# Layer 0 of the next group moved beside the MLP of this one, between the pieces of its second product

## The chip, the cores and the metric

The kernel runs on one core of a Trainium2 chip. The metric is the device time of one execution in microseconds. The runs of the kernel before took 2260.58 to 2263.42 us, with a median of 2262.15.

## The reference

Four layers follow one another on x (64 batches of 64 rows and 256 columns), with a context of the same shape:

```python
def layer0(x_c, x_s):            # channels are the 64 rows, times the 256 columns
    Mn = Wn @ inorm(x_c) + bn;  Mm = Wm @ inorm(x_s) + bm
    A = softmax(Mn.T @ Mm)       # 256 x 256 for each batch
    return Wo @ ((Wl @ x_s + bl) @ A.T) + bo + x_c
def layer1(x, c):                # 32 query heads over 8 key heads of width 8
    return layernorm(softmax(q(x) k(c).T / sqrt(8) + mask) v(c) @ Wo + bo + x) * gamma + beta
def layer2(c, latents):          # 16 heads of width 16, 128 keys: context and latents
    h = attention(latents, concat(c, latents), mask) @ out_w + out_b + latents
    return gelu(rmsnorm(h) @ mlp_w1 + b1) @ mlp_w2 + b2 + latents
def layer3(x, state):            # a recurrence over the 64 rows, 32 heads of 8 x 8
    mixes -> w, k, v, r, g;  s = k v + w s;  out = r (u k v + s_before)
    x1 = x + groupnorm(out) * g @ Wo.T
    return x1 + sigmoid(xr @ Wfr.T) * (relu(xk @ Wfk.T) ** 2 @ Wfv.T)
```

## The kernel before

All is computed in f32. The 64 batches are cut into 8 groups of 8 (512 rows, four tiles of 128 rows). A group passes through layers 0, 1, 2 and the MLP in one block, and through layer 3 in the block after it: group_block(now, before, after) works on layers 0 to 2 of group `now`, on layer 3 of group `before`, and loads the input of group `after`. The blocks are (0, none, 1), then a hardware loop over groups 1 to 6, then (7, 6, none), and (none, 7, none), which holds layer 3 alone. At the end of each block all engines meet, and POOL clears the semaphores.

In a block every engine has its instructions in program order, and the order is written out by hand. A counter of steps runs from 0. Layer 3 is cut into stages (moments, normalize, turn, shift, maa, five mixes with the products between them, 16 scans, center, variance, gate, project and the feed forward stages), and the dictionary `due` gives each a step: the first at 0, the scans at 27 to 42, center at 46, variance at 48, gate at 50, project at 52, the last at 64. The function step() issues the stages due at the present step. Around it, the four steps at the start hold layer 0's first products (mm, mn, ml and the transposes of the context, cT). The loop `for i in range(END)` follows. layer0(i) has eight units of softmax at i = 0 to 7 and their transposes and values up to i = 14. Layer 1's 16 units begin at i = A1 = 14, layer 2's 16 units at A2 = 35, and END is 61. Then come the MLP, eight pieces of the first product (line 579, Gelu at line 936), and the second product as two tiles of four rows of pieces (line 906), with a step after each.

A unit of layer 1 or 2 is a score product (line 714), masked (DVE, 1337), largest (DVE, 1343), subtract (POOL, 1502), exp (ACT, 1049), transposes (855) and a drain (1055, 1057). Four units make a pair (lines 869 and 874), whose totals are inverted by ACT (1067, 1069), divided (DVE, 1358), projected (579) and added (DVE, 1367). A unit of layer 0 is nmax (DVE, 1300), two exponents with sums (ACT, 1039), rden (DVE, 1304), scaling of one half on POOL (1510) and one on ACT (1111), transposes (729), a copy (1310), value (738) and the output product with Wo. Layer 3's scan n is a product on POOL (1464), a column copy (1466), the scan (DVE, 1179), a read-out (DVE, 1191) and a product with `pick` (656).

PSUM has eight banks in three rings: "score" (2 banks: scores of all layers), "turn" (4 banks: all else of layers 0 to 2 and the MLP) and "late" (2 banks: layer 3). fill() waits until the bank's last content was drained, in program order. The input of the next group is loaded by ACT's queue (load_ahead) at the end of layer 2, and its statistics and normalization (normalize_ahead, on DVE, with deviations_ahead on ACT) follow behind the Gelus. The ACT function tables are switched by tables(), line 921, among logarithm and exponent, tanh and exponent, and Gelu.

Of the kernel before, what the change touches and what calls it, by code (L numbers as in the profile page):

```python
# [25 lines left out]
NB = 8  # L26
# [27 lines left out]
def build(nc, a, out):  # L54

    with ExitStack() as ctx:
# [115 lines left out]
        edge = sb("edge", [128, 2, KT, NB])  # L172
        stats3 = sb("stats3", [128, NP, 6])
# [28 lines left out]
        mn = cut(early, 1024, NP, E)  # L202
        mm0 = cut(early, 4096, NP, E)
        mlT = cut(early, 2048, NP, 2, 128)
        mo = cut(early, 3072, NP, E)
# [71 lines left out]
        def normalize_ahead(dve, link):  # L277
# [10 lines left out]
            dve.sem_inc(sig("stats0_ready"), 1)  # L288
            dve.wait_ge(sig("rstd0_ready"), 1)
# [6 lines left out]
        with nc.Block() as block:  # L296
# [137 lines left out]
            def _(dve):  # L434
# [10 lines left out]
                normalize_ahead(dve, link)  # L445
# [70 lines left out]
        A1 = U0 + 6  # L516
        A2 = A1 + UNITS + 5
        END = A2 + UNITS + 10

# [10 lines left out]
        def group_block(now, before, after):  # L530
# [18 lines left out]
            with nc.Block() as block:  # L549
# [22 lines left out]
                def _(pe):  # L572
# [110 lines left out]
                    if now is None:  # L683
                        rest()
                        return


                    step()
                    for q in range(2):
                        product(("mm", q), 512, [(conv["Wm"][:, :], ch[:, 2 * q:2 * q + 2, :])])  # L690
                    for q in range(2):
                        product(("mn", q), 512, [(conv["Wn"][:, :], xh0[:, 2 * q:2 * q + 2, :])])
                    step()
                    for q in range(2):
                        t, full = fill(pe, "turn", ("ml", q))
                        for p in range(2):
                            for s in range(2):
                                ins = mm(t[:, 256 * p + 128 * s:256 * p + 128 * s + 128], c0[:, 2 * q + p, 128 * s:128 * s + 128],
                                         conv["Wl"][:, :], start=True, stop=True)
                        ins.then_inc(full, 1)  # L700
                    step()
                    flip("cT", c0)
                    step()
# [38 lines left out]
                    def layer0(i):  # L742
                        if i < U0 and i % 2 == 0:
                            scores0(i // 2)
# [18 lines left out]
                    def keys1():  # L763
                        pe.wait_ge(sig("cT_ready"), KT)
# [47 lines left out]
                    def between(i):  # L812
                        if i == U0 + 2:
                            keys1()
                        if i == U0 + 6:
                            values1()
                        for h in range(2):
                            if i == 4 * h + 11:
                                pe.wait_ge(sig("x1_ready"), 2 * h + 2)
                                turn_half("x1T", x0, h)  # L820
                            if i == 4 * h + 12:
# [61 lines left out]
                    for i in range(END):  # L883
                        step()
                        layer0(i)
# [10 lines left out]
                    pe.wait_ge(sig("xnT_ready"), 2 * KT)  # L896
                    for n in range(HID // 128):
                        product(("u", n), 512, [(w1[:, k, 128 * n:128 * n + 128], xnT[:, :, k, :]) for k in range(KT)])
                        step()
                    for q in range(2):  # L900
                        t, full = fill(pe, "turn", ("y2", q))
                        for p in (2 * q, 2 * q + 1):
                            for k in range(HID // 128):
                                if p == 0:
                                    pe.wait_ge(sig("gT_ready"), k + 1)
                                ins = mm(t[:, E * (p % 2):E * (p % 2) + E], gT[:, k, 128 * p:128 * p + 128], w2[:, k, :],  # L906
                                         start=k == 0, stop=k == HID // 128 - 1)
                        ins.then_inc(full, 1)
                        step()
# [3 lines left out]
                def _(act):  # L913
# [101 lines left out]
                    if now is None:  # L1015
# [3 lines left out]

                    for q in range(2):  # L1020
                        t, free = take(act, ("mm", q))
                        link(af(mm0[:, 2 * q:2 * q + 2, :].rearrange("p n t -> p (n t)"), t[:, :], ACT.Identity, bias=v("bm")))
                        act.sem_inc(free, 1)
                        act.sem_inc(sig("mm_ready"), 1)
                    step()
                    step()
                    step()
                    for k in range(KT):
                        drain(("cT", k), hT[:, k, :, 0, :], lambda t: batches(t[:, :]), ACT.Identity, "cT_ready")
                    step()  # L1030
# [40 lines left out]
                    def between(i):  # L1071
                        for h in range(2):
                            r = slice(2 * h, 2 * h + 2)
                            if i == 4 * h + 11:
# [27 lines left out]
                    for i in range(END):  # L1102
# [3 lines left out]
                        if i < U0:  # L1106
                            exps0(i)
                        if 1 <= i < U0 + 1:
                            act.wait_ge(sig("rden0_ready"), i)
                            s = soft[:, (i - 1) % SOFT, 256:512]  # L1110
                            af(s, s, ACT.Identity, scale=rden0[:, i - 1, 1:2]).then_inc(sig("p0b_ready"), 1)
# [5 lines left out]
                    if after is not None:  # L1117
                        load_ahead(act, after, lambda: act.wait_ge(sig("xnT_ready"), 2 * KT), lambda: act.wait_ge(sig("xr3_ready"), NP))
                    tables(GELU)
                    for n in range(HID // 128):  # L1120
                        drain(("u", n), gT[:, n, :], lambda t: t[:, :], ACT.Gelu_apprx_tanh, "gT_ready", bias=v("b1", n))
                        step()
                    if after is not None:
                        tables(LOG_EXP)
                        deviations_ahead(act, link)
                    for q in range(2):
                        step()
                    rest()
                    if after is not None:
# [3 lines left out]
                def _(dve):  # L1133
# [143 lines left out]
                    if now is None:  # L1277
# [3 lines left out]

                    step()
                    for q in range(2):
                        t, free = take(dve, ("mn", q))
                        link(ts(flat(mn[:, 2 * q:2 * q + 2, :]), t[:, :], v("bn"), None, ALU.add))
                        dve.sem_inc(free, 1)
                        dve.sem_inc(sig("mn_ready"), 1)
                    step()
                    for q in range(2):
                        t, free = take(dve, ("ml", q))  # L1290
                        link(nc.vector.tensor_copy(mlT[:, 2 * q:2 * q + 2, :, :].rearrange("p n s o -> p (n s o)"), t[:, :]))
                        dve.sem_inc(free, 1)
                        dve.sem_inc(sig("ml_ready"), 1)
                    step()
                    step()

# [272 lines left out]
```

## Time and profile before

| | |
|---|---|
| median of the runs | 2262.15 us |
| profiled execution | 2263.65 us |
| its span | 2261.9 us |
| mean granted clock of TensorE | 0.931 |
| TensorE matmul busy | 1812.2 us (80%) |
| VectorE busy | 1396.9 us (62%) |
| ScalarE busy | 874.9 us (39%) |
| GpSimd busy | 851.3 us (38%) |
| table loads on ScalarE | 55, of 1283 ns each |

An engine is busy while it computes; waits and DMA issues are not counted. The span runs from the first to the last instruction. The granted clock is the share of full speed at which TensorE was run.

### The profile page before, as it was taken

Reading aid. Unit: us, or ns where it says so; the run is one execution under the profiler, and the core shown is the slowest. Engines: PE = TensorE matmul, PEld = TensorE weight load, DVE = VectorE, ACT = ScalarE, POOL = GpSimd, SP = SyncE. Lnnn points to the kernel's source line nnn. Section 1 sums busy time; section 2 is a strip of 40 time slices with the busy share of each in tenths; the row PEclk is TensorE's granted clock in tenths of the full one; section 3 lists DMA queues with packets and bytes.
Section 4 is the critical chain, followed back from the end, with each engine's and each line's share of the span. In section 5 each row is a group of like instructions: output and inputs, shape, how many; then the busy total and the mean of one; then the engine's idle time right before and its main releaser. Section 6 shows DMA issues by size and latency. Waiting matters only on the chain. (4 is left out here: it accounts for less than half of the span.)

```text
span 2261.9 us, 31481 instructions
## 1 busy us (share of the span) xinstructions
PE 1812.2 (80%) x10801; PEld 1095.3 (48%) x10801; DVE 1396.9 (62%) x2337; ACT 874.9 (39%) x1680; POOL 851.3 (38%) x896
## 2 busy tenths in 40 slices
PE   3888877988778787887878878788877888788765
PEld 2465434654356443564445634465434654356413
DVE  3663578635876368754687446873578645875273
ACT  1444442533425334353333533254432543426202
POOL 3531256303752037411374114730266203742060
PEclk9999998999989899998998989999999999989967
DMA  5000011010210102010020101201011010200030
GB/s 155 1 1 24 7 39 39 1 40 1 53 24 2 39 1 63 14 34 8 15 62 1 34 7 26 51 1 40 1 42 35 1 39 1 62 15 10 2 76 9
DMA packets 73515, 60.84 MB, mean 27 GB/s; under 512 B 38888, under 2 KB 56440, under 8 KB 73336
## 3 DMA queue, kind: packets, MB, share of 16 engines
q1 hardware_dynamic: 49592, 41.70, 8.5%
q10 hardware_dynamic: 23200, 16.85, 2.5%
q8 instruction: 98, 1.61, 0.3%
q14 instruction: 81, 0.66, 0.1%
q0 software_dynamic: 544, 0.03, 0.0%
HBM read 20.28 MB, written 4.19 MB: 11 GB/s over the span
## 5 line engine op out<-in xcount | busy, mean ns | idle before, releaser
L1502 POOL TENSOR_TENSOR soft_ring<-soft_ring,seg_max 128x512 f32<-128x512 f32 x256 | 326.7, 1284 | 495.9 <-DVE seg_max L1343 495.8
L1049 ACT ACTIVATE soft_ring<-soft_ring 128x512 f32<-128x512 f32 x256 | 160.9, 628 | 413.3 <-POOL soft_ring L1502 406.8
L656 PE MATMUL bank<-late,pick 128*128 128x512 f32 x256 | 160.8, 715 | 99.9 <-DVE late L1191 99.7
L1337 DVE SCALAR_TENSOR_TENSOR soft_ring<-bank,mask 128x512 f32<-128x512 f32 x256 | 164.6, 684 | 105.0 <-PE bank L714 94.4
L1464 POOL TENSOR_TENSOR late<-late 128x520 f32<-128x520 f32 x128 | 197.4, 1542 | 71.2 <-DMA late<-late 49.9
L1179 DVE TENSOR_TENSOR_SCAN late<-late 128x520 f32<-128x520 f32 x128 | 188.0, 1468 | 9.3 <-DVE xr L1367 2.2
L1343 DVE TENSOR_REDUCE seg_max<-soft_ring 128x8 f32<-128x512 f32 (+1 forms) x256 | 169.4, 677 | 8.9 <-DVE early L1400 1.9
L1510 POOL TENSOR_SCALAR soft_ring<-soft_ring,rden 128x256 f32<-128x256 f32 x64 | 59.1, 924 | 305.3 <-DVE rden L1304 305.3
L855 PEld LDWEIGHTS bank<-ident,soft_ring 128*128 128x128 f32 x1024 | 121.5, 147 | 108.2 <-issue 86.8
L714 PE MATMUL bank<-early 64*128 64x512 f32 (+1 forms) x512 | 123.3, 583 | 58.6 <-ACTq L1042 55.2
L855 PE MATMUL bank<-ident,soft_ring 128*128 128x128 f32 x1024 | 164.4, 290 | 5.8 <-ACT soft_ring L1049 5.5
L579 PE MATMUL bank<-late,maa 128*128 128x512 f32 (+1 forms) x224 | 126.1, 680 | 23.4 <-DVEq L1171 19.3
L579 PE MATMUL bank<-wo,early 128*128 128x256 f32 x512 | 130.2, 399 | 11.0 <-DVEq L1361 10.9
L1191 DVE TENSOR_TENSOR late<-late 128x512 f32<-128x512 f32 x128 | 135.8, 1061 | 0.3 <-PE bank L656 0.3
L921 ACT ACT_TABLE_LOAD x55 | 70.6, 1283 | 163.4 <-issue 102.9
L579 PE MATMUL bank<-early,w 128*128 128x512 f32 x256 | 113.6, 602 | 7.4 <-ACT early L1098 7.4
L656 PEld LDWEIGHTS bank<-late,pick 128*128 128x128 f32 x256 | 46.5, 216 | 150.2 <-DVE late L1191 108.6
L579 PEld LDWEIGHTS bank<-wo,early 128*128 128x128 f32 x512 | 97.9, 199 | 32.5 <-DVEq L1361 14.3
L906 PE MATMUL bank<-w,early 128*128 128x256 f32 x512 | 111.8, 379 | 0.0
L936 ACT ACTIVATE early<-bank,vec 128x512 f32<-128x512 f32 x96 | 66.0, 687 | 107.1 <-PE bank L579 104.3
L906 PEld LDWEIGHTS bank<-w,early 128*128 128x128 f32 x512 | 97.3, 190 | 16.6 <-issue 3.8
L714 PEld LDWEIGHTS bank<-early 64*128 64x128 f32 x512 | 48.9, 211 | 113.6 <-issue 111.9
(242 smaller groups left out, 3390.1 us busy)
## 6 DMA issues: line engine op xcount, KB each, us to landing
late<-late SPq DMA_DIRECT2D x128, 260.0 KB, 3.0
c<-in_ctx ACTq DMA_DIRECT2D x8, 512.0 KB, 3.8
x<-in_x ACTq DMA_DIRECT2D x8, 512.0 KB, 6.0
out_x<-late SPq DMA_DIRECT2D x8, 512.0 KB, 4.9
mask<-in_mask_Bx1xSxS_ff ACTq DMA_DIRECT2D x16, 128.0 KB, 4.8
w<-in_L_xattn_mlp_w ACTq DMA_DIRECT2D x2, 1024.0 KB
mask<-in_mask_BxS_ik SPq DMA_DIRECT2D x8, 256.0 KB, 3.5
wkv<-in_L_xattn_kv_w ACTq DMA_DIRECT2D x1, 512.0 KB
```

Of the source, the lines that this page charges most:

```text
L579: ins = mm(t[0:lhsT_cols(lhsT), 0:cols], lhsT, rhs, start=n == 0, stop=n == len(terms) - 1)
L656: mm(t[:, :], pick[:, j, :], rs[:, j % 2, :], start=j == 0, stop=j == HS - 1).then_inc(full if j == HS - 1 else sig("rs_used"), 1)
L714: ins = mm(t[:, width * n:width * n + width], lhsT, rhs, start=True, stop=True)
L855: ins = tr(t[:, 128 * n:128 * n + 128], soft[:, u % SOFT, 128 * n:128 * n + 128], ident[:, :])
L906: ins = mm(t[:, E * (p % 2):E * (p % 2) + E], gT[:, k, 128 * p:128 * p + 128], w2[:, k, :], start=k == 0, stop=k == HID // 128 - 1)
L1049: af(soft[:, u % SOFT, :], soft[:, u % SOFT, :], ACT.Exp).then_inc(sig("exp"), 1)
L1179: nc.vector.tensor_tensor_scan(sj[:, n % 2, :], wP[:, k, :, :].rearrange("p b t -> p (b t)"), aj[:, n % 2, :], 0.0, ALU.mult, ALU.add).the ...
L1191: tt(batches(rs[:, n % 2, :]), batches(rT[:, k, :]), sj[:, n % 2, :].rearrange("p (b t) -> p b t", t=LP)[:, :, 0:L], ALU.mult).then_inc(si ...
L1337: stt(out=cuts(u, soft[:, u % SOFT, :]), in0=cuts(u, t[:, :]), scalar=HD1 ** -0.5 if u < UNITS else 1.0 / HD2, in1=mask.unsqueeze(1).broad ...
L1343: nc.vector.tensor_reduce(seg_max[:, u % SOFT, 0:KVH if u < UNITS else 4], cuts(u, soft[:, u % SOFT, :]), X, ALU.max).then_inc(sig("max"), 1)
L1464: tt(aj[:, n % 2, :], kP[:, k, :, :].rearrange("p b t -> p (b t)"), vj[:, n % 3, :], ALU.mult).then_inc(sig("kv_done"), 1)
L1502: tt(s, s, seg_max[:, u % SOFT, 0:segs].unsqueeze(2).broadcast_to([128, segs, 512 // segs]), ALU.subtract).then_inc(sig("sub"), 1)
```

## The change

The block no longer starts with layer 0. A block works on layers 1 and 2 and the MLP of `now`, on layer 3 of `before` and on layer 0 of `after`. Layer 1's units begin at i = A1 = 3 and A2 is 24, END 50; the keys, values and queries of layer 1 stand at i = 0 to 2. After that come 25 slots, each with one step(): slots 0 to 7 hold a piece of the first MLP product, slots 8 to 15 half of a row tile of the second (four of eight terms each, one bank for each row tile in place of one for two), and layer 0 of the next group has its first products at slots 7 to 9 and its units from slot 10 on. The stages of layer 3 keep their steps, so gate (step 50) now falls into slot 0. The statistics of the next input are taken at slot 4 and its normalization at slot 6. Tiles mn, mlT and mo have other places so that they don't share memory with gT. POOL copies two columns of the context's transpose to `edge_now` at the start of a block, since layer 0 now overwrites them in it, and ACT waits for that. A block (none, none, 0) with layer 0 alone of group 0 comes first. The waits on x1_ready and cT_ready are gone, since the border of the block lies between.

```diff
-        A1 = U0 + 6
+        A1 = 3
         A2 = A1 + UNITS + 5
         END = A2 + UNITS + 10
+        HIDDEN = HID // 128
+        AHEAD = 10
+        SLOTS = AHEAD + U0 + 7
+        def slots(now, after):
+            if after is None:
+                return range(2 * HIDDEN + 1)
+            return range(AHEAD - 3 if now is None else 0, SLOTS)
...
# TensorE
+                        if i == -3:
+                            if now is not None:
+                                pe.wait_ge(sig("ahead_ready"), 2 * NP)
+                            (products mm and mn)
+                        if i == -2: (products ml)
+                        if i == -1:
+                            flip("cT", c0)
...
-                        if i == U0 + 2:
+                        if i == 0:
                             keys1()
-                        if i == U0 + 6:
+                        if i == 2:
                             values1()
...
+                    def hidden_out(p, late_half):
+                        if not late_half:
+                            fill(pe, "turn", ("y2", p))
+                        b, _ = place["y2", p]
+                        for k in range(4 * late_half, 4 * late_half + 4):
+                            if p == 0:
+                                pe.wait_ge(sig("gT_ready"), k + 1)
+                            ins = mm(banks[b][:, 0:E], gT[:, k, 128 * p:128 * p + 128], w2[:, k, :], start=k == 0, stop=k == HIDDEN - 1)
+                        if late_half:
+                            ins.then_inc(sig(f"bank{b}_full"), 1)
+                    for s in slots(now, after):
                         step()
+                        if now is not None and s < HIDDEN:
+                            hidden(s)
+                        if now is not None and HIDDEN <= s < 2 * HIDDEN:
+                            hidden_out((s - HIDDEN) // 2, s % 2)
+                        if after is not None:
+                            layer0(s - AHEAD)
...
# ScalarE
+                    for s in slots(now, after):
                         step()
+                        if now is not None and s < HIDDEN:
+                            tables(GELU)
+                            drain(("u", s), gT[:, s, :], lambda t: t[:, :], ACT.Gelu_apprx_tanh, "gT_ready", bias=v("b1", s))
+                        if now is not None and after is not None and s == 6:
+                            tables(LOG_EXP)
+                            deviations_ahead(act, link)
+                        if after is not None:
+                            layer0(s - AHEAD)
...
# VectorE
+                    for s in slots(now, after):
                         step()
+                        if now is not None and after is not None:
+                            if s == 4:
+                                statistics_ahead(dve, link)
+                            if s == 6:
+                                normalize_ahead(dve)
+                        if now is not None and s % 2 == 0 and HIDDEN + 2 <= s <= 2 * HIDDEN:
+                            hidden_added((s - HIDDEN) // 2 - 1)
+                        if after is not None:
+                            layer0(s - AHEAD)
...
+        group_block(None, None, 0)
         group_block(0, None, 1)
```

## Rows read from the trace of the kernel before

**Rows 1.** Timeline of TensorE, first product of four blocks: start us, us, engine, line, [idle before].
```profile
44.84 2.19 PE L579 MATMUL bank<-early,conv_Wm 128*128 128x512 f32 x3 [2.28 <-PEq L483]
...
227.27 1.95 PE L579 MATMUL bank<-early,conv_Wm 128*128 128x512 f32 x4 [1.98 <-PEq L483]
...
495.85 2.07 PE L579 MATMUL bank<-early,conv_Wm 128*128 128x512 f32 x2 [6.11 <-issue]
...
767.22 1.22 PE L579 MATMUL bank<-early,conv_Wm 128*128 128x512 f32 x1 [6.03 <-issue]
```

**Rows 2.** Windows of one turn of the loop; columns in the first line.
```profile
core 0: us, PE busy (x) PEld busy (x) DVE busy (x) ACT busy (x) POOL busy (x), PEclk, DMA share, GB/s
495.90:595.50 99.60, 82.63 (x421) 41.53 (x422) 59.47 (x107) 41.29 (x89) 32.57 (x32) 0.93 0.07 14
595.50:671.00 75.50, 56.02 (x303) 34.03 (x302) 65.39 (x84) 21.30 (x40) 55.32 (x48) 0.91 0.18 41
...
676.70:733.40 56.70, 49.67 (x498) 38.37 (x496) 33.72 (x61) 35.30 (x67) 12.80 (x16) 1.00 0.01 1
733.40:761.20 27.80, 27.79 (x96) 18.13 (x96) 8.27 (x28) 8.57 (x12) 0.36 (x2) 1.00 0.23 67
```

**Rows 3.** Line 1179 (the scans) in two windows: duration ns min/median/max, first and last start.
```profile
L1179 DVE TENSOR_TENSOR_SCAN late<-late x12: 1230/1407/1760, 593.1 to 636.3; 128x520 f32<-128x520 f32 x12
...
L1179 DVE TENSOR_TENSOR_SCAN late<-late x4: 1225/1230/1231, 645.9 to 660.9; 128x520 f32<-128x520 f32 x4
```

**Rows 4.** Windows of the first block, up to layer 1's scores and from there on.
```profile
44.80:84.50 39.70, 29.19 (x179) 19.05 (x179) 17.98 (x36) 16.44 (x46) 10.85 (x12) 0.83 0.03 8
84.50:195.90 111.40, 92.51 (x888) 64.27 (x887) 67.51 (x119) 56.16 (x109) 47.40 (x52) 0.98 0.00 1
```

**Rows 5.** Groups by line and form, one turn: busy us, mean ns | idle before.
```profile
L1337 DVE SCALAR_TENSOR_TENSOR soft_ring<-bank,mask 128x512 f32<-128x512 f32 x32 | 20.6, 685 | 14.4 <-PE bank L714 13.1 <-DVE early L1358 0.9 <-DVE xr L1367 0.3
L855 PE MATMUL bank<-ident,soft_ring 128*128 128x128 f32 x128 | 20.4, 289 | 0.6 <-ACT soft_ring L1049 0.6
...
L579 PE MATMUL bank<-wo,early 128*128 128x256 f32 x64 | 16.3, 400 | 1.4 <-DVEq L1361 1.4
...
L1343 DVE TENSOR_REDUCE seg_max<-soft_ring 128x4 f32<-128x512 f32 x16 | 10.5, 677 | 0.6 <-DVE late L1197 0.2 <-DVE early L1358 0.2
L714 PE MATMUL bank<-early 64*128 64x512 f32 x32 | 9.4, 662 | 0.4 <-DVE soft_ring L1337 0.4
...
L809 PE MATMUL bank<-wkv,hT 128*128 128x256 f32 x32 | 7.6, 388 | 0.0
...
L579 PE MATMUL bank<-hT,wkv 128*128 128x512 f32 x16 | 7.2, 593 | 0.0
L1350 DVE TENSOR_TENSOR qring<-early,hmask 128x512 f32<-128x512 f32 x8 | 6.8, 857 | 1.1 <-DVE early L1415 0.5 <-DVE early L1358 0.2 <-DVE xr L1367 0.2
...
L869 PE MATMUL bank<-early,ones 128*32 128x256 f32 x64 | 4.3, 385 | 0.0
...
L1264 DVE SCALAR_TENSOR_TENSOR late<-late,vec 128x512 f32<-128x512 f32 x4 | 2.8, 748 | 0.1
```

**Rows 6.** Timeline of TensorE at the end of layer 2 in the first block.
```profile
186.24 1.12 PE L874 MATMUL bank<-early,ones 128*32 128x128 f32 x32
187.14 1.13 PE L874 MATMUL bank<-early 128*32 128x128 f32 x32
...
194.26 0.66 PE L760 MATMUL bank<-ident,c 128*128 128x128 f32 x4 [2.50 <-DVE c L1380]
195.85 1.22 PE L579 MATMUL bank<-early,w 128*128 128x512 f32 x1 [0.93 <-ACT early L1098]
```

**Rows 7.** Timeline of ScalarE behind the last Gelu, and of VectorE for the next input.
```profile
748.29 1.28 ACT L921 ACT_TABLE_LOAD   x1 [0.19 <-ACT early L936]
...
480.02 1.38 DVE L292 TENSOR_SCALAR early<-x,mv,rstd 128x256 f32<-128x256 f32 x4
```

**Rows 8.** Line 1502 (subtract): first block, and layer 2 units beside scans.
```profile
L1502 POOL TENSOR_TENSOR soft_ring<-soft_ring,seg_max x32: 1038/1042/1417, 88.6 to 177.9; 128x512 f32<-128x512 f32 x32
...
L1502 POOL TENSOR_TENSOR soft_ring<-soft_ring,seg_max x7: 1040/1899/1902, 646.0 to 674.8; 128x512 f32<-128x512 f32 x7
```

More of the change, by code:

```diff
@@ L682, in _ @@
                     step, rest = beside(layer3)
-                    if now is None:
+                    if now is None and after is None:
                         rest()
                         return
[L688 to L703, printed above, removed]
                     HALVES = (slice(0, 64), slice(64, 128))
@@ L881, in project @@
                         product(("out", c), E, [(attended[:, c % 2, n, :], wo1[:, n, :] if c < NP else wo2[:, n // 2, n % 2, :]) for n in range(4)])
-                    for i in range(END):
+                    for i in range(END) if now is not None else ():
                         step()
-                        layer0(i)
                         if unit(i) >= 0 and unit(i) % 2 == 0:
@@ L1100, in between @@
                                 act.sem_inc(free, 1)
-                    for i in range(END):
+                    for i in range(END) if now is not None else ():
                         step()
@@ L1105, in _ @@
                             turned(unit(i - 3))
[L1106 to L1111, printed above, removed]
                         between(i)
@@ L1420, in between @@
                                 one_query(b)
-                    for i in range(END):
-                        layer0(i)
+                    for i in range(END) if now is not None else ():
                         if unit(i) >= 0 and unit(i) % 2 == 0:
@@ L1489, in _ @@
                     step, rest = beside(layer3)
-                    if now is None:
+                    if now is None and after is None:
                         rest()
                         return
-                    for _ in range(4):
-                        step()
+                    if now is not None:
+                        for s in range(2):
+                            ins = nc.gpsimd.tensor_copy(edge_now[:, s, :, :], hT[:, :, :, 0, s])
+                        link(ins)
+                        pool.sem_inc(sig("edge_saved"), 1)
                     def subtract(u):
@@ L1503, in subtract @@
                            ALU.subtract).then_inc(sig("sub"), 1)
-                    for i in range(END):
+                    for i in range(END) if now is not None else ():
                         step()
-                        if i < U0:
-                            pool.wait_ge(sig("rden0_ready"), i + 1)
-                            s = soft[:, i % SOFT, 0:256]
-                            ts(s, s, rden0[:, i, 0:1], None, ALU.mult).then_inc(sig("p0_ready"), 1)
                         if unit(i) >= 0:
```

164 lines of the change are left out of this document (82 added, 82 removed).

## The prediction

> **What bounds the kernel now.** I read the windows of one turn of the loop first, then the timeline of TensorE at the block borders, then durations by line. One turn lasts 767.22 - 495.85 = 271.4 us [rows 1]. In the windows [rows 2] TensorE is busy 82.6 of the first 99.6 us (83%), 56.0 of the 75.5 us from 595.5 to 671 (74%), 49.7 of the 56.7 us up to the MLP (88%), and all of the 27.8 us of the MLP; then 6.03 us of nothing stand ahead of the next turn [rows 1]. VectorE has 65.4 of 75.5 us in the window of the scans and about 60% in the windows on both sides of it. So there are three kinds of stretch: TensorE alone (the MLP), VectorE (the scans), and stretches in which in-order queues wait for each other with TensorE at 83 to 88%. About 50 us of a turn find TensorE idle; no work leaves the kernel, so the change can only gain from these 50 us.
>
> **What moves.** Layer 3 keeps its due steps (0 to 64, the scans at 27 to 45), but a turn now counts: steps 0 to 49 are layers 1 and 2, steps 50 to 74 the MLP slots, with layer 0 of the next group from slot 7. Before, steps 0 to 17 held layer 0, layer 1's units ran at steps 18 to 33 and layer 2's at 39 to 54. Now they run at 3 to 18 and 24 to 39. I price five stretches of a turn, each from one event to the next. Before they were 97.2 (start to the first scan, 593.1), 67.8 (first to last scan start, 660.9 [rows 3]), 72.5 (to the MLP, 733.4), 27.8 and 6.0.
>
> **Stretch 1, start to the first scan.** Layer 0 leaves. Alone in the first block it and some 3.7 us of keys and queries keep TensorE busy 29.2 us at a granted clock of 0.83 [rows 4], so I take 24 us for it. In come, up to step 26, seven more units' scores (9.4 x 7/16 = 4.1), ten more turned units (20.4/32 = 0.64 each, 6.4), three more pairs (two products of 1.07 each, 6.4), four output projections (16.3/8 each, 8.1), half of layer 2's keys and values (3.6 + 3.8), its queries at half the keys' work (1.8), a pair of transposes (0.7) and two pairs of layer 2 scores (at layer 1's 9.4/8 each, 2.3) [rows 5]: 37.1 us. Groups that follow each other overlap in the rows (one starts at 186.24 and takes 1.12, the next starts at 187.14 [rows 6]); some 25 groups by 0.1 to 0.2 us, and I take 35 net. TensorE then has 82.6 - 24 + 35 = 94 us of work here. Its share is between what this stretch has now, 83%, and the 88% of the window before the MLP [rows 2], where units, pairs and layer 3 products also share the steps. I take 88%, the nearer in mix of work, since the ping-pong of layer 0 over two score banks has left: 94/0.88 = 107, less the 2.4 us by which the first scan starts before 595.5: 104.5, and 105 with a start in which keys, transposes and queries wait for one another. Bounds: 96.5 (a share of 95%, well above any mixed window) and 111 (83%). So +8.
>
> **Stretch 2, the scans.** VectorE sets it: 67.8 us here. Of its other work between scan 0 and scan 15 there were ten units, now 13: +3 x (0.685 + 0.677) = +4.1; two more spread queries (0.857 each) +1.7; a divide, an add and some normalizing less, about -3.0 (lighter instructions than a unit each) [rows 5]. Net +2.8, and with the 8% that the stretch lasts beyond its own list, 71. Bounds: 68 and 75.
>
> **Stretch 3, last scan to the MLP.** Before, the end of layer 3 (center to the last product) filled the waits of layer 2's end. Now layer 2 ends at step 49 with only center and variance beside it. In the first block, where nothing else runs, the last pair product starts at 186.24 and the MLP at 195.85: 9.6 us of chain (totals, divide, project, add, square, table load, root, scale, transpose, drain) [rows 6]. Ahead of it stand two bare scan steps (4 us); inside it 3.9 us of center and variance on TensorE and ScalarE, in order ahead of the projection and of the last drain. Sum 17.5; bounds 13.6 and 20. So -55.
>
> **Stretch 4, the slots.** TensorE's work is the MLP, 27.8 [rows 2], layer 3's Wo, Wfk, Wfr and Wfv (each twice one MLP piece of 27.8/16 = 1.74, 14 in all, and 1.2 for transposes) and layer 0's 24, for a sum of 67. Two stalls come in. First, slot 7: layer 0's first products wait for the normalized inputs, whose deviation sits in ScalarE's queue behind the Gelu of piece 6. Table load 1.28 and two short activations 0.5, then eight normalizations 2.8 [rows 7], against 2.8 us of TensorE work in between (a transpose stage and piece 7): after the semaphores some 2 to 3.5 us. Second, slots 8 to 10: the context's second transpose needs a bank that holds the first MLP output, and VectorE drains it only behind a shift stage (six instructions of about 0.75, 4.4 [rows 5]) and two copies (1.4): some 2 us. Against that, slots 16 to 24 hold the tail of layer 0: exponent, scaling, transpose, copy, value, output, of which TensorE fills the most; some 2.5 us are bare. 67 + 3 + 2 + 1 = 73 to VectorE's last add; bounds 67 and 80. The extra table loads (Gelu, logarithm, Gelu, logarithm, tanh in the slots, and totals between tanh stages) are about six of 1.28; ScalarE, near 40% busy, hides them except in slot 7. Before, layer 0 was not here, so +45. The copies of the edge (POOL, 0.8) lie beside waits and cost nothing; if not, 0.8.
>
> **Stretch 5, the border.** Barrier and clear stay: 5.5 from VectorE's last instruction.
>
> **Sum.** 105 + 71 + 17.5 + 73 + 5.5 = 272, against 271.4: the idle time changes place rather than size. +0.6 for each of seven groups (six turns and the last full block): +4.2.
>
> **The ends.** A block with layer 0 of group 0 alone is new. The first block before lasted 227.27 - 44.84 = 182.4 us [rows 1], of which 39.7 up to layer 1's scores and 111.4 from there to the MLP [rows 4]. After: layer 0 alone 37.2 + a border of 2.3; then a start of 10.5, again 111.4, slots without layer 3 60, border 2: 223.4, or +41. The block of the last group has no layer 0 beside its MLP: 24 us of work, both stalls and a bit of tail, -30.3. Ends together +10.7.
>
> The profiled execution took 2263.65 (span 2261.9 and 1.75 around it), the runs' median is 2262.15. I add to the median: 2262.15 + 10.7 + 4.2 = 2277. Break-even is a turn shorter by 10.7/7 = 1.5 us. Forecast: slower by 0.7%.
>
> **Rivals.**
> (a) Faster. Layer 0 fits into the slots without either stall (-5.5) and center and variance hide in layer 2's closing chain (-3.9): a turn of 262.6, -8.8 x 7 + 10.7, so 2211. For it: the closing chain leaves TensorE gaps of 2.50 and 0.93 us in the first block [rows 6] into which 3.9 us nearly fit. Against it: layer 3's pieces stand in the queue at fixed places. It decides from a turn below 269.9.
> (b) Two engines over one path. Layer 2's subtract on POOL takes 1.042 us when no scan runs and 1.899 us (median) beside scans [rows 8]; scans beside layer 2 units start (660.9 - 645.9)/3 = 5.0 us apart, the first twelve, mostly beside layer 1 units or none, 3.93 apart [rows 3]. With all 13 units beside scans now layer 2's: 13 x 5.0 + 2 x 2.8 + 4.3 of other work = 75 in place of 71, a turn of 276, and 2262.15 + 10.7 + 32 = 2305. Against it: the five-microsecond steps also carry layer 2 preparations already counted.
> The Trainium skill (SBUF — State Buffer, section "SBUF: two separate sides") says that VectorE with two SBUF inputs and GpSimd lock a shared port pair for a whole instruction and the loser blocks. The stretched subtract agrees with it.
> (c) Crowding. Mixes, layer 1 units and pairs in the same steps keep TensorE at 83% as over all of the present stretch: 111, a turn of 278, and 2319. For it: a masked score ahead of a mix in VectorE's queue delays both bank rings. Against it: layer 0's ping-pong has left, and most of today's gap in this stretch lies before its layer 1 units.
>
> **Numbers.** Forecast 0.50 (own range 2256 to 2298, from turns of 269 to 275), (a) 0.24, (b) 0.12, (c) 0.14. What can be told from no change is about 0.2%, 4.5 us. Faster: (a) and a tenth of the forecast case, 0.29; same 0.08; slower 0.63. The range leaves out the outer half of (a) and of (c): 2218 to 2318.
>
> **What would show it.** From a turn's start the first scan at 105 (97.2 now), 71 between first and last scan, 17.5 to the first MLP product, 73 from there to the border. TensorE idle 2 to 3.5 us ahead of the first Wm product, waiting for VectorE. A new block of some 37 us. Wrong would be: a first scan before 100 or after 110, a slot stretch near 67, or scans at 5.0 throughout.

## The result, and the profile after

The changed kernel took 2309.87 us (2309.04 to 2310.41), the one before 2262.62: a ratio of 1.021, 95% interval 1.0192 to 1.0228. It is slower by 47 us, where 15 were forecast. The sign held, and the time lies in the widest range given (2218 to 2318), but above the forecast case's own (2256 to 2298); the size of the change is three times the forecast.

The first part of the profile page, after (busy us, share of the span, instructions). No TensorE instruction was added, yet its busy time is 41 us up on 1812.2, nearly the whole growth of the span from 2261.9 to 2307.2; its idle time stays at 450 to 454 us.

```profile
span 2307.2 us, 31550 instructions
...
PE 1853.2 (80%) x10801; PEld 1117.1 (48%) x10801; DVE 1438.6 (62%) x2353; ACT 937.7 (41%) x1729; POOL 868.9 (38%) x904
```

Windows of one turn after (540.64 to 817.18, 276.5 us): start to first scan, the scans, last scan to the MLP, the slots, and the whole turn.

```profile
core 0: us, PE busy (x) PEld busy (x) DVE busy (x) ACT busy (x) POOL busy (x), PEclk, DMA share, GB/s
540.60:651.40 110.80, 94.48 (x540) 51.26 (x540) 68.83 (x115) 49.52 (x81) 38.23 (x45) 0.92 0.06 12
651.40:717.70 66.30, 51.50 (x407) 34.24 (x408) 63.93 (x73) 24.42 (x47) 59.09 (x47) 0.88 0.21 48
717.70:734.60 16.90, 13.80 (x104) 8.28 (x102) 6.74 (x11) 8.67 (x19) 2.09 (x5) 0.97 0.00 0
734.60:812.00 77.40, 67.94 (x296) 44.76 (x296) 39.60 (x93) 34.90 (x71) 7.55 (x9) 0.96 0.08 25
540.60:817.20 276.60, 227.73 (x1346) 138.56 (x1346) 179.13 (x289) 117.51 (x217) 107.32 (x107) 0.92 0.10 24
```

The same whole turn, and its first stretch, in the kernel before:

```profile
495.90:593.10 97.20, 81.21 (x413) 40.45 (x413) 57.39 (x104) 40.34 (x87) 30.24 (x29) 0.93 0.06 12
...
495.90:767.20 271.30, 221.80 (x1344) 135.15 (x1344) 172.75 (x288) 109.66 (x211) 104.60 (x106) 0.95 0.11 25
```

Against the stretches of the prediction, where slots and border are one number:

| stretch, us | before | forecast | after |
|---|---|---|---|
| start to first scan | 97.2 | 105 | 110.8 |
| the scans | 67.8 | 71 | 66.3 |
| last scan to the MLP | 72.5 | 17.5 | 16.9 |
| MLP or slots, and border | 33.8 | 78.5 | 82.6 |
| turn | 271.4 | 272 | 276.5 |

A turn is 5.1 us longer rather than 0.6. The table shows one turn; over the six turns the first stretch took 109.5 to 112.0 us, and the third 15.6 or 16.9, the 15.6 behind a long first stretch. Seven times 5.1 is 36; the other 9.6 of the span's 45.3 are the ends (10.7 forecast).

The slots on TensorE, after (start, us, line, [idle before <- releaser]):

```profile
734.57 5.40 PE L593 MATMUL bank<-early,w 128*128 128x512 f32 x8 [2.23 <-ACT early L1126]
739.80 3.62 PE L609 MATMUL bank<-t_Wo,late 128*128 128x256 f32 x16
743.26 8.75 PE L593 MATMUL bank<-early,w 128*128 128x512 f32 x20
...
752.71 1.88 PE L593 MATMUL bank<-early,w 128*128 128x512 f32 x4
758.19 1.98 PE L593 MATMUL bank<-early,conv_Wm 128*128 128x512 f32 x4 [3.60 <-DVE early L295]
...
766.97 0.60 PE L601 MATMUL bank<-ident,c 128*128 128x128 f32 x4
769.72 0.88 PE L601 MATMUL bank<-ident,c 128*128 128x128 f32 x4 [2.15 <-DVEq L1459]
770.39 3.40 PE L918 MATMUL bank<-w,early 128*128 128x256 f32 x8
```

Both forecast stalls are there, 3.60 us ahead of Wm and 2.15 ahead of the context's second transpose. But the reader should look at what follows a gap: the first two MLP pieces take 5.40 us, where twice 1.88 less an overlap is 3.6, and the second-product piece behind the transposes takes 3.40 in place of 1.89. I had priced the gaps and not the work behind them. In both places the granted clock was half (two windows, columns as above: the last three are granted clock, DMA share and GB/s):

```profile
735.90:739.30 3.40, 3.40 (x5) 1.33 (x4) 1.32 (x3) 1.42 (x2) 0.00 (x0) 0.50 0.92 253
770.00:773.40 3.40, 3.40 (x12) 2.75 (x10) 0.00 (x0) 1.88 (x2) 0.00 (x0) 0.50 0.02 5
```

Behind the longest gap, 3.60 us, the clock did not fall at once: Wm took 1.98 us and Wn 1.88.

### The profile page after: what moved, and what is told of

The parts are those of the page before. It is cut to its first block and busy times, and to the rows that moved or that the text cites. A ratio compares the mean times of both kernels' runs of the same rounds, so it can differ in the third digit from the quotient of the medians.

```text
span 2307.2 us, 31550 instructions
## 1 busy us (share of the span) xinstructions
PE 1853.2 (80%) x10801; PEld 1117.1 (48%) x10801; DVE 1438.6 (62%) x2353; ACT 937.7 (41%) x1729; POOL 868.9 (38%) x904
## 5 line engine op out<-in xcount | busy, mean ns | idle before, releaser
L1488 POOL TENSOR_TENSOR late<-late 128x520 f32<-128x520 f32 x128 | 211.8, 1654 | 52.1 <-DMA late<-late 49.8
L670 PE MATMUL bank<-late,pick 128*128 128x512 f32 x256 | 165.4, 734 | 72.8 <-DVE late L1214 72.5
L866 PEld LDWEIGHTS bank<-ident,soft_ring 128*128 128x128 f32 x1024 | 128.9, 152 | 131.3 <-issue 91.4
L866 PE MATMUL bank<-ident,soft_ring 128*128 128x128 f32 x1024 | 171.4, 297 | 12.2 <-ACT soft_ring L1077 11.9
L593 PE MATMUL bank<-late,maa 128*128 128x512 f32 (+1 forms) x224 | 134.5, 726 | 43.5 <-DVE late L1235 22.9
L593 PE MATMUL bank<-early,w 128*128 128x512 f32 x256 | 124.5, 639 | 16.6 <-ACT early L1126 16.6
L918 PE MATMUL bank<-w,early 128*128 128x256 f32 x512 | 128.7, 399 | 0.0
L710 PE MATMUL bank<-early 64*128 64x512 f32 (+1 forms) x512 | 112.6, 538 | 18.6 <-DVE soft_ring L1355 11.7
L593 PE MATMUL bank<-wo,early 128*128 128x256 f32 x512 | 123.5, 384 | 3.0 <-DVEq L1379 2.9
L670 PEld LDWEIGHTS bank<-late,pick 128*128 128x128 f32 x256 | 47.6, 221 | 118.1 <-DVE late L1214 82.6
L1319 DVE TENSOR_REDUCE nmax<-bank 128x2 f32<-128x512 f32 x64 | 43.2, 687 | 94.9 <-PE bank L710 91.8
L710 PEld LDWEIGHTS bank<-early,qring 64*128 64x128 f32 x1024 | 73.9, 218 | 48.7 <-issue 48.7
```

The costliest lines, as they stand in the source:

```text
L593: ins = mm(t[0:lhsT_cols(lhsT), 0:cols], lhsT, rhs, start=n == 0, stop=n == len(terms) - 1)
L670: mm(t[:, :], pick[:, j, :], rs[:, j % 2, :], start=j == 0, stop=j == HS - 1).then_inc(full if j == HS - 1 else sig("rs_used"), 1)
L710: ins = mm(t[:, width * n:width * n + width], lhsT, rhs, start=True, stop=True)
L866: ins = tr(t[:, 128 * n:128 * n + 128], soft[:, u % SOFT, 128 * n:128 * n + 128], ident[:, :])
L918: ins = mm(banks[b][:, 0:E], gT[:, k, 128 * p:128 * p + 128], w2[:, k, :], start=k == 0, stop=k == HIDDEN - 1)
L1488: tt(aj[:, n % 2, :], kP[:, k, :, :].rearrange("p b t -> p (b t)"), vj[:, n % 3, :], ALU.mult).then_inc(sig("kv_done"), 1)
```

## The experiments

The times below are medians; "off" is against 2309.9 unless said otherwise. The expectations set theory A (a gap costs its own length) against theory B (it also costs half clock in work near it), and others as they come. The stretches of one turn of most runs are in a table at the end of the section. A filler is a product whose result is overwritten.

**x1: the gap ahead of Wm out.**

```diff
# ScalarE, behind step() of the slot
+                        if now is not None and after is not None and s == 4:
+                            tables(LOG_EXP)
+                            deviations_ahead(act, link)
-                        if now is not None and after is not None and s == 6:
-                            tables(LOG_EXP)
-                            deviations_ahead(act, link)
# VectorE
-                            if s == 4:
+                            if s == 3:
                                 statistics_ahead(dve, link)
```

> The changed kernel took 2309.9 us. Here the statistics of the next input are taken at slot 3 and its deviations at slot 4, where the logarithm table is loaded for layer 3 anyway, so that slot 7 waits for nothing and two table loads a turn go. Theory A (stalls at fixed places): the 3.60 us gap ahead of the first Wm product goes in seven blocks, 2309.9 - 25 = 2285. Theory B (the clock): the gap goes and TensorE is not granted half clock behind it either (a stretch of 3.4 us at half, worth 1.7 us), 2309.9 - 37 = 2273. Theory C (the slots are bounded by their work, what is gained is waited for later): above 2303.

Measured 2279.39 (ratio to before 1.0079, 1.0062 to 1.0096): 30.5 off. Wm starts without a wait (the timeline of x1):

```profile
739.77 1.88 PE L593 MATMUL bank<-early,w 128*128 128x512 f32 x4
741.49 1.91 PE L593 MATMUL bank<-early,conv_Wm 128*128 128x512 f32 x4
...
753.69 0.66 PE L601 MATMUL bank<-ident,c 128*128 128x128 f32 x4 [1.98 <-DVEq L1459]
754.18 1.89 PE L918 MATMUL bank<-w,early 128*128 128x256 f32 x8
```

The second gap is still there (1.98 us), and yet the piece behind it is back at 1.89 us. In place of the first gap TensorE now waits 1.02 and 0.61 us near it. The edit also takes twelve table loads out of the run (92 in place of 104), so it doesn't price the gap alone.

It gained more than the gap in seven blocks (25), less than the gap with a stretch of half clock (37). A full turn is 3.3 shorter, seven times 23; the rest came ahead of the loop's second turn, by a cause that no run shows. Theory C is out.

**x2: the gap ahead of the second transpose out.**

```diff
-                            fill(pe, "turn", ("y2", p))
+                            fill(pe, "turn" if p else "score", ("y2", p))
```

> The changed kernel, with the first row tile of the second MLP product in a bank of the score ring, so that the context's second transpose doesn't wait for VectorE to drain it. Theory A: the gap of 2.15 us goes in seven blocks, 2309.9 - 15 = 2295. Theory B: also the piece behind it, 3.40 us in place of 1.89, is back at full clock, 2285. Theory C: no change.

Measured 2287.33 (1.012, 1.0103 to 1.0138): 22.5 off, near theory B's 25. The two transposes run as one group and the piece behind them is back at its 1.9 us (the timeline of x2):

```profile
760.00 1.04 PE L601 MATMUL bank<-ident,c 128*128 128x128 f32 x8
761.08 1.99 PE L918 MATMUL bank<-w,early 128*128 128x256 f32 x8
```

**x3: the gaps stay, but TensorE is kept busy in four of them** by products whose results are overwritten.

```diff
-                    def product(tile, cols, terms, ring="turn"):
+                    def product(tile, cols, terms, ring="turn", extra=0, wait=None):
                         t, full = fill(pe, ring, tile)
+                        for n in range(extra):
+                            mm(t[:, 0:512], ident[:, :], w1[:, 0, 0:512], start=True, stop=True)
+                        if wait is not None:
+                            pe.wait_ge(*wait)
```

> The changed kernel plus products whose results are overwritten (0.87 us each at full clock), in four gaps of TensorE in each turn: three ahead of maa, four ahead of bonus, three ahead of the first Wm product, two ahead of the first MLP product. They are no longer than the gaps, and stand ahead of the waits. Theory A: no gap gets shorter, so no change or a little slower, 2310 to 2320. Theory B: TensorE keeps its full clock behind these gaps; busy time of the real work falls by up to 2 to 3 us a turn, 2290 to 2298.

Measured 2283.6 (1.0095, 1.0078 to 1.0112): 26.3 off, although TensorE does 93 products more and the data that it waits for come no sooner. The mean granted clock is 0.934, where after has 0.909 and before 0.931. The timeline of x3 at the same place as above:

```profile
726.69 1.88 PE L593 MATMUL bank<-w,ident 128*128 128x512 f32 x4
729.09 3.70 PE L597 MATMUL bank<-early,w 128*128 128x512 f32 x8 [0.51 <-ACT early L1130]
...
747.25 2.74 PE L593 MATMUL bank<-w,ident 128*128 128x512 f32 x6
751.01 1.98 PE L597 MATMUL bank<-early,conv_Wm 128*128 128x512 f32 x4 [1.02 <-DVE early L295]
...
762.53 0.66 PE L605 MATMUL bank<-ident,c 128*128 128x128 f32 x4 [2.15 <-DVEq L1463]
763.03 1.89 PE L922 MATMUL bank<-w,early 128*128 128x256 f32 x8
```

A filler is two instructions here. The first MLP pieces take 3.70 in place of 5.40, and the gap of 2.15 is unchanged, yet the piece behind it takes 1.89 in place of 3.40. Theory A, gaps alone, falls: it expected no gain. The slots run at a granted 1.00 here (the window from 728.9 to 803), against 0.96. Only the slots gain: the first stretch stays at 110.2 although its granted clock rose from 0.92 to 0.95.

**x4: layer 0 behind the MLP, beside nothing.**

```diff
-        AHEAD = 10
+        AHEAD = 19
```

> The changed kernel with layer 0 nine slots later (AHEAD 19), so that it starts when the second MLP product is done and runs beside nothing. It tells what the overlap of the slots is worth. By my walk through the slots (layer 0 alone 37 us, the rest of the slots 44) the stretch takes 81 in place of 77 us: 2309.9 + 7 x 4 = 2338. If the MLP hides layer 0's waits as the change means it to (15 us a turn), 2415. If the interleaving only costs, below 2310.

Measured 2338.57 (1.0334, 1.0317 to 1.0351), 28.7 more, as the count in the expectation had it (2338). So all of the overlap in the slots is worth 4.1 us a turn (28.7 over seven; 3.4 in the one turn of the table). The MLP keeps TensorE busy by itself [rows 2], and what runs beside it has little idle time to fill.

**x5: x1 and x2 together.**

> The changed kernel with both edits that were tried singly (statistics at slot 3 and deviations at slot 4; first row tile of the second product in the score ring). Singly they took 30.5 and 22.5 us off 2309.9. If each takes its own gap and the low clock behind it, the sum: 2257, under the kernel before. If the low clock is what both share, or what one gains the next wait takes, 2265 to 2279.

Measured 2269.35 (2261.24 to 2271.11; 1.0026, 1.0014 to 1.0038): 40.5 off, not 53. The plain sum was wrong, and the other reading, that the two share something, held. Each of them alone had already cured the same piece (3.40 us back to 1.89 in x1 and to 1.99 in x2), so its 1.5 us can't be won twice. Five blocks of the changed kernel have the slow piece: that is 7.5 of the 12.5 us that are missing. The turn of the table, with slots of 75.4, is a lucky one. The same gap of 2.23 us ahead of the first MLP pieces has full clock behind it in this turn and half clock in the next, whose slots take 77.1 us (the timeline of x5):

```profile
723.63 3.70 PE L593 MATMUL bank<-early,w 128*128 128x512 f32 x8 [2.23 <-ACT early L1126]
...
993.44 5.40 PE L593 MATMUL bank<-early,w 128*128 128x512 f32 x8 [2.23 <-ACT early L1126]
```

The mean clock, 0.913, is below x1's 0.920: the low clock partly moved elsewhere.

**x6: x5 with three of x3's fillers** (ahead of maa, bonus and the first MLP product).

```diff
-                            product((stage, k), 512, [(block8[:, :, :], ruk[:, k, :])], "late")
+                            product((stage, k), 512, [(block8[:, :, :], ruk[:, k, :])], "late",
+                                    0 if k else 4, (sig("ruk_ready"), k + 1))
```

> x5 with the overwritten products in the remaining three gaps (three ahead of maa, four ahead of bonus, two ahead of the first MLP product). Theory B (the clock): another 15 to 20 us off x5, about 2240. Theory A (gaps alone): as x5 or up to 5 us slower.

Measured 2259.4 (0.9986, 0.9977 to 0.9996), 10 off x5, which is less than the 15 to 20 expected, and not the nothing of theory A.

**x7: x6 with POOL's mask conversion 14 steps later.**

```diff
-                        if i == A1:
+                        if i == A1 + 14:
                             pool.wait_ge(sig("mask2_in"), 16)
```

What suggested it stands in the timelines of VectorE and POOL, after:

```profile
556.18 1.16 DVE L1234 TENSOR_TENSOR late<-late 128x512 f32<-128x512 f32 x1
557.38 1.10 DVE L1235 SCALAR_TENSOR_TENSOR late<-late,vec 128x512 f32<-128x512 f32 x1
558.40 1.52 DVE L1234 TENSOR_TENSOR late<-late 128x512 f32<-128x512 f32 x1
```

```profile
556.75 1.17 POOL L1541 TENSOR_TENSOR xr<-x,row 128x256 f32<-128x256 f32 x1
557.89 1.49 POOL L1538 TENSOR_TENSOR early<-early,kvmask 128x512 f32<-128x512 f32 x1
559.46 2.26 POOL L1552 TENSOR_SCALAR mask<-mask 128x512 f32<-128x512 int32 x1
```

and before, where POOL stood idle at that time (VectorE):

```profile
506.77 0.68 DVE L1211 TENSOR_TENSOR late<-late 128x512 f32<-128x512 f32 x1
507.49 0.75 DVE L1212 SCALAR_TENSOR_TENSOR late<-late,vec 128x512 f32<-128x512 f32 x1
```

> x6 with POOL's conversion of layer 2's mask (2.26 us) 14 steps later, away from layer 3's shift, whose instructions last up to 1.52 us in place of 0.68 beside it. If that contention holds up maa, 4 to 8 us off x6. If the shift is stretched by the other POOL work there anyway, within 3 us of x6.

Measured 2255.36 (0.9971, 0.9959 to 0.9982), 4 off x6; the two ranges overlap (2252.9 to 2263.0 and 2252.8 to 2259.3), so a small gain is likely and not shown.

**x8: the kernel before, with fillers** (five products in the bank of maa, ahead of layer 0's second scores, and two ahead of bonus).

```diff
                     def layer0(i):
+                        if i == 2 and before is not None:
+                            t, _ = fill(pe, "late", "maaA")
+                            for _ in range(5):
+                                mm(t[:, :], ident[:, :], w1[:, 0, 0:512], start=True, stop=True)
```

> The kernel before, with overwritten products in two of its own gaps (five in the 5.4 us between layer 0's first and second scores, two ahead of bonus). Theory B holds for any kernel: half clock of 6.8 us behind the first gap goes, 2 to 4 us a turn, 2236 to 2250. If the low clock matters only in the changed kernel, 2260 to 2270.

Measured 2251.49 (0.9961, 0.9947 to 0.9975), 11 off the kernel before and at the edge of what theory B gave. The product of maa behind the first filled gap took 5.32 us before, and takes 1.98 and 1.90 in x8 (the first line is of the kernel before, the others of x8):

```profile
513.55 5.32 PE L579 MATMUL bank<-late,maa 128*128 128x512 f32 x8
...
503.42 1.13 PE L723 MATMUL bank<-early 64*128 64x256 f32 x8 [0.83 <-ACTq L1055]
504.49 1.98 PE L628 MATMUL bank<-late,maa 128*128 128x512 f32 x4
506.40 1.90 PE L583 MATMUL bank<-late,maa 128*32 128x512 f32 x4
```

So low clock behind gaps was already a cost there before the change. But the mean granted clock stayed where it was (0.932 against 0.931): what the first stretch gained in clock (0.97 against 0.93) was lost further on in the turn. By which path the 11 us came is not shown.

**x9: VectorE takes layer 3's stage ahead of the masks**, in x7, up to step 18.

```diff
+                        if i < A1 + UNITS:
+                            step()
                         if unit(i) >= 0 and unit(i) % 2 == 0:
                             masked(unit(i))
...
-                        step()
+                        if i >= A1 + UNITS:
+                            step()
```

> x7 with VectorE taking layer 3's stage ahead of the masked scores and maxima of the same step, up to step 18 (before: behind them). Theory D (crowding in the first stretch comes from VectorE's order: a mix stage waits behind masks that wait for scores, and TensorE's next late product waits for the mix): the waits ahead of maa and of the second mix fall, the first scan comes 3 to 5 us earlier in a turn, 2230 to 2238. If the stretch is set by the sum of TensorE's work, or layer 1's units now wait in their turn, 2252 to 2262.

Measured 2258.14 (0.9982, 0.9972 to 0.9991): no gain. The first stretch took 112.2 (111.6 as the mean of five turns, 111.0 in x7). The edit did what it was meant to: the wait of 2.19 us for VectorE ahead of the second mix is gone. A longer one, for a bank that ScalarE drains, came in its place (the timeline of x9):

```profile
574.18 3.78 PE L597 MATMUL bank<-late,t_Wk 128*128 128x512 f32 x4 [3.88 <-ACTq L961]
```

So VectorE's order alone doesn't make the crowding, and theory D falls.

**x10: x8 with fillers in the last block too**, seven ahead of Wo and four ahead of Wfk.

```diff
+                                for _ in range(7):
+                                    mm(t[:, :], ident[:, :], w1[:, 0, 0:512], start=True, stop=True)
                                 pe.wait_ge(sig("ogT_ready"), KT)
```

> x8 (2251.5 us) with overwritten products also in the last block, where layer 3 runs alone: seven ahead of Wo's first tile (a gap of 6.65 us, and then 5.97 us of work that takes 3.7 at full clock) and four ahead of Wfk's (3.78 us, then 6.24 in place of 3.7). By the clock theory 4 to 5 us once: 2247. If the clock is not what stretches them: 2251 or more.

Measured 2251.17 (0.9957, 0.994 to 0.9974): as x8. The timeline shows what the total hides:

```profile
2205.92 6.28 PE L679 MATMUL bank<-w,ident 128*128 128x512 f32 x14 [0.96 <-ACTq L962]
2212.03 1.89 PE L683 MATMUL bank<-t_Wo,late 128*128 128x256 f32 x8
2213.76 1.89 PE L599 MATMUL bank<-t_Wo,late 128*128 128x256 f32 x8
2220.44 1.97 PE L591 MATMUL bank<-ident,late 128*128 128x128 f32 x8 [4.79 <-DVE late L1185]
2222.47 5.87 PE L579 MATMUL bank<-w,ident 128*128 128x512 f32 x8
2228.18 3.60 PE L583 MATMUL bank<-late,t_Wfk 128*128 128x512 f32 x8
```

Wo takes 3.6 us in place of 5.97 and Wfk 3.60 in place of 6.24, so the clock did stretch them; but the four fillers ahead of Wfk themselves ran at half clock behind a gap of 4.79, took 5.87 us and overran a gap of 3.78 by 2.1. From the seventh to the eighth store it is 2.9 us shorter than x8, which is what these numbers add up to. That the total shows nothing of it comes from the loop's first turn, where the two kernels are the same: it took 267.5 us at a granted 0.96 here, and 263.8 at 0.98 in x8's profile.

**x11: half of the k, v, r and g products left out**, on the changed kernel (the second half of each sum over the input columns).

```diff
-                            square(w, lambda k: xm[:, (n + 1) % 2, k, :])
+                            for m in range(KT):
+                                product((stage, m), 512, [(wt[w][:, 0, 128 * m:128 * m + 128], xm[:, (n + 1) % 2, 0, :])], "late")
```

> The changed kernel (2309.9 us; 110.8 us from a turn's start to the first scan) with the second half of the sum left out of layer 3's k, v, r and g products: eight matmuls fewer for TensorE in that stretch, 7.0 us, with all evictions and waits as they are. Theory E (the stretch is set by TensorE's work, and my share of 88% was too high): it shrinks by 6 to 8 us in each turn, 7 x 7 = 49 off, 2261. Theory F (it is set by the chain of evictions and mixes): 0 to 2 us a turn, 2296 to 2310.

Measured 2279.15 (1.007, 1.0053 to 1.0086): 30.7 off. The first stretch fell from 110.8 to 106.8, so 4.0 of 7.0 us removed (TensorE's busy time there fell by 5.8): between the two theories. TensorE's work counts for a bit more than half there; the rest went into waits.

**x12: tables ahead**, in x7.

```diff
# ScalarE, in the loop over i, ahead of exps(unit(i))
+                        if before is not None and i in (5, 11, 19):
+                            tables(TANH)
```

> x7 (2255.4 us) with ScalarE's tanh table loaded one unit earlier at three places of the first stretch (ahead of the exponent in steps 5, 11 and 19 rather than at the tanh itself), so that maa, td and g don't wait 1.28 us for it. Theory G (ScalarE's table loads, 104 in place of 55, lie on the path to the first scan): 1.3 to 4 us a turn, 2228 to 2246. If TensorE finds other work meanwhile: within 4 us of 2255.

Measured 2236.4 (2230.71 to 2237.0; ratio to before 0.9882, 0.9866 to 0.9899): 19 off x7, the best version of all and 1.2% faster than the kernel before. What it moves can be seen on ScalarE, after: the two tanh instructions of maa stand behind an exponent that waits for POOL, and only then behind the table.

```profile
565.56 0.63 ACT L1077 ACTIVATE soft_ring<-soft_ring 128x512 f32<-128x512 f32 x1 [0.57 <-POOL soft_ring L1528]
566.21 1.28 ACT L941 ACT_TABLE_LOAD   x1
567.50 0.60 ACT L956 ACTIVATE late<-bank 128x512 f32<-128x512 f32 x1
```

In x12 the load stands in the free time of ScalarE two exponents earlier:

```profile
542.28 0.63 ACT L1081 ACTIVATE soft_ring<-soft_ring 128x512 f32<-128x512 f32 x1 [3.40 <-POOL soft_ring L1534]
542.93 1.28 ACT L945 ACT_TABLE_LOAD   x1
```

The number of loads is the same in x7 and x12 (92); only their place differs. On TensorE the wait between the products of maa fell from 2.17 us to 0.76 (x7, then x12):

```profile
557.68 1.98 PE L597 MATMUL bank<-late,maa 128*128 128x512 f32 x4 [2.17 <-ACTq L962]
...
549.51 1.99 PE L597 MATMUL bank<-late,maa 128*128 128x512 f32 x4 [0.76 <-ACTq L962]
```

The distance from the first to the sixth store, over five, fell from 269.5 in x7 to 266.5: 3.0 us a turn. As the mean of five turns, 1.9 of it is ahead of the first scan and 1.3 ahead of the MLP (0.7 and 1.3 in the turn of the table below). Which load bites where is not settled, only that their place does. Of the 20.3 us between the two profiles, 3.2 came ahead of the loop, where the edit does nothing; so some 17 of those 20 are its own.

| us in one turn | to first scan | scans | to MLP | slots, border | turn |
|---|---|---|---|---|---|
| after | 110.8 | 66.3 | 16.9 | 82.6 | 276.5 |
| x1 | 110.6 | 66.4 | 16.9 | 79.3 | 273.2 |
| x2 | 110.8 | 66.4 | 16.8 | 78.9 | 272.9 |
| x3 | 110.2 | 66.3 | 16.9 | 79.3 | 272.7 |
| x4 | 111.4 | 66.4 | 16.8 | 85.3 | 279.9 |
| x5 | 112.4 | 66.4 | 16.8 | 75.4 | 270.9 |
| x7 | 110.4 | 66.4 | 16.9 | 75.1 | 268.8 |
| x11 | 106.8 | 66.4 | 16.9 | 82.7 | 272.8 |
| x12 | 109.7 | 66.4 | 15.6 | 75.3 | 267.0 |

## Why the prediction was right in sign and wrong in size

**What bounds, and the ends: right.** The idle time of a turn did not shrink, and the ends cost 9.6 us (10.7 forecast).

**The first stretch: mis-sized by 5.8 us.** The failed step is the share of 88%. I had 94 us of work for TensorE, and the window has 94.5 busy; but its share is 85% (94.48 of 110.8), near the 83% of this stretch before [rows 2], which was the bound of case (c). The stretch came out as case (c) had it (111), and past the 110 that was named as a sign of being wrong. The reason that I gave for 88% was that the ping-pong of layer 0 had left. But other waits came: the longest are on the shift ahead of maa (2.82 us), on the second mix (2.19) and on bonus (4.01). That a layer 3 chain and a layer 1 chain now start together is my explanation of them, and no run shows it. The clock is not what stretches it: x3 raised it there from 0.92 to 0.95 and won 0.6 us. x9 shows that VectorE's order alone is not what makes the waits, x11 that of 7.0 us of TensorE's work taken out 4.0 come back as time, x12 that the place of ScalarE's table loads is worth 1.9 us of it (on top of x7).

**The table loads: costed at nothing, wrongly.** I counted six more in a turn, let ScalarE at 40% busy hide them outside slot 7, and named no work between each load and its reader. There are 104, where the table of the profile before has 55. A load in front of a tanh that TensorE waits for was on the path although the engine is 41% busy: loading three of them earlier gave 19 us on x7, at an unchanged number of loads (92).

**The scans: over-priced by 4.7.** 66.3 us came out where 71 were forecast. VectorE's own list was priced nearly right: 60.5 us busy before, 63.9 after, where +2.8 was forecast. What failed was to keep its idle time, 7.3 us of the 67.8 before (which is 12% on top of the list, not the 8% of the prediction): 2.4 us of it were left. Why it shrank, no run shows. Case (b) did not come about.

**Last scan to the MLP: right** (16.9 against 17.5), with a stall of 2.23 us ahead of the MLP in it.

**The slots: mis-sized by 4.1.** Of the 82.6 us TensorE was busy for 67.9 (67 in the sum), the two stalls took 3.60 and 2.15 (3 and 2), five short waits in the tail of layer 0 took 3.2 (the sum has 1, although the text ahead of it says 2.5), and the border 5.7 (5.5). The 67.9 hold a term that the sum left out, so the work itself was priced 2.3 too high: TensorE ran at half of its clock for a while, 5.40 - 3.70 = 1.7 us in the first pieces and 3.40 - 1.89 = 1.5 in the piece behind the transposes (after against x3). The granted clock shows full or half speed (2.4 or 1.2 GHz), the mean over the run fell from 0.931 to 0.909, and x3 brings it back to 0.934 with every wait in place and takes 26.3 us off. x1, x2 and x3 show that the stalls with the low clock near them are worth 22.5 to 30.5 us of the run.

**Its sum.** 5.8 - 4.7 - 0.6 + 4.1 = 4.6 us a turn, seven times 32, less 1.1 for the ends: 31 of the 32.8 us between 2277 and 2309.9. That the error of the scans offset most of that of the first stretch is luck.

**What stays open.** What makes the waits of the first stretch, beside the table loads, and which of ScalarE's three loads x12 gained by.

## What to carry to other kernels

Work moved beside an engine that is already full gains little there (x4: 4.1 us a turn for a whole layer), and where it came from other waits remain; price the place that it leaves and the borders that it adds. Here two gaps of some 2 us on TensorE had 1.5 and 1.7 us more in the work behind them, beside their own length, in most turns though not in all; so look at the durations behind each gap, not at the idle column alone. Two cures that share such a piece don't add up (x5). A table load is priced by what waits for the function behind it, and is best put ahead of an instruction that waits anyway.

## What the runs showed of the hardware

After a gap of 2.23 us TensorE's next eight instructions took 5.40 us in place of 3.70, in five of the seven blocks of the changed kernel that have this gap, and in three of the seven in x5. After one of 2.15 us eight took 3.40 in place of 1.89 (more than 3.2 in five of six turns) at a place where an earlier gap of 3.60 us had ended some 9 us before, and that one had full clock right behind it. Filling or removing the earlier gap cured the later piece, though its own gap stayed at 2.15 us (x3) or 1.98 (x1). So what a gap does to the clock depended on more than its length. Fillers are no free cure: at half clock they last 1.47 us each (5.87 for four) and can outlast the gap (x10).

VectorE's operation on two SBUF tensors took 1.16 and 1.52 us beside POOL's work and 0.68 with POOL idle. The Trainium skill (SBUF — State Buffer, section "SBUF: two separate sides") tells of a port pair that GpSimd shares with VectorE's instructions on two SBUF inputs, and that one of them holds for a whole instruction. The rows agree with it, but the gain from moving one of POOL's instructions away, 4 us in x7, is within what these runs can't tell from none.
